# Sharing the scaled residual add of a sandwich block between ScalarE and VectorE

## The chip, the cores and the metric

One core of one Trainium2 chip runs the kernel. The metric is the device time of one execution in microseconds (us). Engines are called as in the profile: PE is TensorE, DVE is VectorE, ACT is ScalarE, POOL is GpSimd, SP is SyncE.

## The reference, cut to what matters

```python
x = L0_attn_x                                     # (4, 1024, 512) f32
x = x + _layernorm(attention(_layernorm(x)))      # windowed attention on tokens of 16 channels
x = x + _layernorm(ffn(_layernorm(x)))            # ffn: silu(x@w_gate*s_gate) * (x@w_up*s_up) @ w_down*s_down
```

The change concerns the end of the second line. The attention's rows of 512 values are normalised (mean and variance of each row) and added to x. The layernorm of that sum is what the feed-forward part reads.

## The kernel before

The 4096 rows are worked on in 8 tiles of 512 rows; in the feed-forward layout a tile is 128 partitions by 4 blocks (`q`, `NQ` = 4) of 512 values. The attention of a tile works in another layout (windows on partitions), so its result goes through device memory: `att_store` (SP) writes it to `scratch` and loads it back into `o1`, in the row layout. The order of 16-element pieces in a row of `o1` is not that of `xr` (the block of x itself): `norm1_add` reads `o1` as `(ae h w)` and adds to `xr` as `(h ae w)`, with w = 16, h = 4, ae = 8.

The steps of a tile t that matter here, by name, engine and line:

- `ffn_norm1`: DVE takes statistics of the four blocks of `o1` (L1158) and forms mean and variance (L976 to L984). POOL turns them into the inverse deviation `frs[:, 0, 0]` and the shift `frs[:, 0, 1]` with three small instructions (L826, L828, L830); the last one raises `f_rs`.
- `norm1_add`: DVE waits for `f_rs` and for `xr`, and adds `o1 * frs` to `xr` with 16 SCALAR_TENSOR_TENSOR instructions of 128 elements, four for each block (L1173).
- `ffn_norm2`: DVE takes statistics of `xr` (L1149), again DVE then POOL.
- `norm2_apply`: ACT writes the normalised rows over `o1` (L736); `fx_transpose`: PE transposes them (L593), ACT and DVE split them into two f16 parts `xhi` and `xlo` (L741, L1183).
- `keep_x1`: ACT adds the shift `frs[:, 0, 1]` to `xr` later (L792).
- The feed-forward part of the tile before runs meanwhile in 16 steps m: `gate` and `up` on PE (L599), silu on ACT (L766), `fuse` on DVE (L1190), `fuse_hi` on ACT (L772), `fuse_lo` on POOL (L926), `down` on PE (L622), three steps later. `ps_gate` and `ps_up` have one bank each, so PE's next `gate` waits for the silu and its next `up` for the `fuse`.

One list of steps gives every engine its order (`body_steps`, `attention_steps`, `walk`); each engine runs its own part of it strictly in that order. In the steady tiles `ffn_norm1` has slot 40, `norm1_add` slot 41, `token_bias` (POOL, L843) and `ffn_norm2` slot 42, `norm2_apply` slot 44. Three slots are one step m. So ACT's order about the change is: copy of the last `qkv` (L713), [slot 41], silu of step 14, `fuse_hi` of step 13, and so on. The first tile runs `norm1_add` ahead of any feed-forward step (`BEFORE`), behind ACT's eight `qkv` copies; the last one has it at slot 43 (`LAST2`). `norm1_add` of tile 1 is in `FIRST`, those of tiles 2 to 5 in the hardware loop over `MIDDLE`, that of tile 6 in the copy of `MIDDLE` behind the loop.

Of the kernel before, what the change touches and what calls it, by code (L numbers as in the profile page):

```python
# [10 lines left out]
WIN = 8  # L11
# [10 lines left out]
NQ = ROWS // P  # L22
# [10 lines left out]
ALU = mybir.AluOpType  # L33
ACT = mybir.ActivationFunctionType
# [12 lines left out]
def sandwich_kernel(nc, x, qkv_w, conv_w0, conv_b0, conv_w1, conv_b1, proj_w, proj_b, ln_w, ln_b,  # L47
                    w_gate, w_up, w_down, s_gate, s_up, s_down, scratch, out):
    with ExitStack() as ctx:
        def sb(name, shape, dt=F32):  # L50
            return ctx.enter_context(nc.sbuf_tensor(name, shape, dt))
# [4 lines left out]
        def sem(name):  # L56
            return ctx.enter_context(nc.semaphore(name))
# [60 lines left out]
        o1 = sb("o1", [P, NQ, W])  # L118
# [4 lines left out]
        frs = sb("frs", [P, 3, 2, NQ])  # L123
# [69 lines left out]
        f_stats = sem("f_stats")  # L193
        f_pool = sem("f_pool")
        f_rs = sem("f_rs")
        xr_sum = sem("xr_sum")
        fx_done = sem("fx_done")
        fx_tr = sem("fx_tr")
# [153 lines left out]
        p, a, b, c = (0, 0), (0, 1), (1, 0), (1, 1)  # L352
# [94 lines left out]
        def _(sp):  # L447
            def load_xb(t, *_):

                need(sp, xt_tr, 4 * t)
                need(sp, xl_done, 4 * t)
                for h in range(WIN):
                    src = x_att[t, h] if isinstance(t, int) else x_att[bass.ds(t, 1), h].rearrange("o k p w -> (o k) p w")
                    sp.dma_start(xb[:, h, :], src).then_inc(s_xb, 16)

            def load_xr(t, *_):

                need(sp, x1_done, t)
                if isinstance(t, int) and t == 0:  # L460
                    sp.wait_ge(w_cast, 2 * KB)
                for hi in range(2):
                    if isinstance(t, int):
                        src = x_ffn[t // 2, t % 2, hi]
                    else:
                        src = x_ffn[bass.ds(t // 2, 1), bass.ds(t % 2, 1), hi].rearrange("b s lo k n -> (b s lo) k n")
                    dst = xr[:, 2 * hi:2 * hi + 2, :].rearrange("p q n -> p (q n)")
                    sp.dma_start(dst, src).then_inc(s_xr, 16)

            def att_store(t, *_):  # L470

                if isinstance(t, int) and t == 0:
                    sp.wait_ge(w_cast, CASTS)

                need(sp, s_out, 32 * (t - 1))
                dst = r_store[t] if isinstance(t, int) else r_store[bass.ds(t, 1)].rearrange("o p c n -> (o p) c n")
                src = ratt[:].rearrange("p c h w -> p c (h w)")
                for hi in range(2):

                    sp.wait_ge(ratt_done, 4 * t + 3 + hi)  # L480
                    part = slice(hi * HB, hi * HB + HB)
                    sp.dma_start(dst[:, part], src[:, part]).then_inc(s_ratt[hi], 16)
                if isinstance(t, int) and t == 1:

                    sp.wait_ge(fx_tr, KB)
                for hi in range(2):

                    sp.wait_ge(s_ratt[hi], 16 * t + 16)
                    for g in range(2):
                        rows = r_load[t, hi, g] if isinstance(t, int) \  # L490
                            else r_load[bass.ds(t, 1), hi, g].rearrange("o r ae n -> (o r) ae n")
                        sp.dma_start(o1[:, 2 * hi + g, :].rearrange("p (ae n) -> p ae n", ae=2 * NQ),
                                     rows).then_inc(s_o1[hi], 16)
# [196 lines left out]
        def _(act):  # L690
# [35 lines left out]
            def square(at, u, ut, uq):  # L726
# [3 lines left out]
                nc.scalar.activation(csq[:, part].rearrange("p h t c -> p (h t c)"),  # L730
                                     cent[:, part].rearrange("p h t c -> p (h t c)"), ACT.Square).then_inc(sq_done, 1)

            def norm2_apply(t, ut, uq):
                act.wait_ge(f_rs, 2 * t + 2)
                for q in range(NQ):
                    nc.scalar.activation(o1[:, q, :], xr[:, q, :], ACT.Identity, bias=frs[:, 1, 1, q:q + 1],  # L736
                                         scale=frs[:, 1, 0, q:q + 1]).then_inc(fx_done, 1)
# [71 lines left out]
            for dst, src in ((sgate, s_gate), (sup, s_up)):  # L809
                act.dma_start(dst[:], src.rearrange("(m p) -> p m", p=P),  # L810
                              allow_slow_non_contiguous=True).then_inc(s_const2, 16)
            walk(act, {"ln1_apply": ln1_apply, "xt_transpose": xt_transpose, "qkv": qkv, "exp": exp,
                       "cat_transpose": cat_transpose, "square": square, "cent_std": cent_std,
                       "norm2_apply": norm2_apply, "fx_transpose": fx_transpose,
                       "gate": gate, "fuse_hi": fuse_hi, "finish_apply": finish_apply,
                       "finish_apply_last": finish_apply_last, "keep_x1": keep_x1,
                       "cast": cast})
# [153 lines left out]
        def _(dve):  # L971
# [190 lines left out]
            def norm1_add(t, ut, uq):  # L1162

                dve.wait_ge(f_rs, 2 * t + 1)
                dve.wait_ge(s_xr, 32 * t + 32)
                for q in range(NQ):

                    sums = xr[:, q, :].rearrange("p (h ae w) -> p h ae w", h=WIN // 2, w=C)  # L1170
                    rows = o1[:, q, :].rearrange("p (ae h w) -> p h ae w", h=WIN // 2, w=C)
                    for h in range(WIN // 2):
                        a = nc.vector.scalar_tensor_tensor(sums[:, h], rows[:, h], frs[:, 0, 0, q:q + 1], sums[:, h],  # L1173
                                                           ALU.mult, ALU.add)
                    a.then_inc(xr_sum, 1)

            def ffn_norm2(t, ut, uq):
                dve.wait_ge(xr_sum, NQ * t + NQ)
# [117 lines left out]
            def scales(t, ut, uq):  # L1296
# [11 lines left out]
                       "softmax": softmax, "pv": pv, "pv_norm": pv_norm,  # L1308
                       "attn_out": attn_out, "proj": proj, "cent_var": cent_var, "cent_out": cent_out,
                       "ffn_norm1": ffn_norm1, "norm1_add": norm1_add, "ffn_norm2": ffn_norm2,  # L1310
                       "fx_transpose": fx_transpose, "fuse": fuse_step, "pv_sum": pv_sum,
                       "finish": finish, "blocks": blocks, "scale_sums": scale_sums, "scale_pow2": scale_pow2,
# [29 lines left out]
```

## Time and profile before

| | us |
|---|---|
| median of 3 runs (lowest, highest) | 1413.1 (1411.92, 1414.27) |
| span of the profiled execution | 1412.0 |
| DVE busy | 1243.1 (88%) |
| PE busy | 1044.9 (74%) |
| POOL busy | 765.3 (54%) |
| ACT busy | 523.5 (37%) |

Busy time counts an instruction from its start to its end, and that includes any time it is held back inside by another engine. The timeline view gives start, duration, engine, line, operation and shapes, and in square brackets the idle time of the engine before it and who ended that.

### The profile page before, as it was taken

Reading aid. Unit: us, or ns where it says so; the run is one execution under the profiler, and the core shown is the slowest. Engines: PE = TensorE matmul, PEld = TensorE weight load, DVE = VectorE, ACT = ScalarE, POOL = GpSimd, SP = SyncE. Lnnn points to the kernel's source line nnn. Section 1 sums busy time; section 2 is a strip of 40 time slices with the busy share of each in tenths; the row PEclk is TensorE's granted clock in tenths of the full one; section 3 lists DMA queues with packets and bytes.
Section 4 is the critical chain, followed back from the end, with each engine's and each line's share of the span. In section 5 each row is a group of like instructions: output and inputs, shape, how many; then the busy total and the mean of one; then the engine's idle time right before and its main releaser. Section 6 shows DMA issues by size and latency. Waiting matters only on the chain. (4 is left out here: it accounts for less than half of the span.)

```text
span 1412.0 us, 14344 instructions
## 1 busy us (share of the span) xinstructions
PE 1044.9 (74%) x4483; PEld 531.0 (38%) x4483; DVE 1243.1 (88%) x1716; ACT 523.5 (37%) x790; POOL 765.3 (54%) x492
## 2 busy tenths in 40 slices
PE   5524368777887688868787778876887688678896
PEld 3312244343443343434343334433444244233442
DVE  4999999999899999999899998999899999975313
ACT  2235335332452434414253324524344143523332
POOL 2555336565576555765456644765557664754322
PEclk9756669889898899979898899988899799889998
DMA  4100200103001210102101030012101020012000
GB/s 128 30 0 13 77 6 24 30 1 89 1 16 45 60 31 1 38 21 59 30 3 57 0 89 1 15 45 59 30 1 46 15 60 1 7 53 60 7 24 30
DMA packets 70266, 46.07 MB, mean 33 GB/s; under 512 B 39616, under 2 KB 64192, under 8 KB 70208
## 3 DMA queue, kind: packets, MB, share of 16 engines
q1 hardware_dynamic: 65344, 45.10, 11.5%
q10 hardware_dynamic: 4864, 0.32, 0.2%
q8 instruction: 22, 0.36, 0.1%
q14 instruction: 36, 0.29, 0.1%
HBM read 28.63 MB, written 16.78 MB: 32 GB/s over the span
## 5 line engine op out<-in xcount | busy, mean ns | idle before, releaser
L599 PE MATMUL ps_up<-xhi,wu 128*128 128x512 f16 x512 | 218.8, 427 | 145.1 <-DVE fuse L1190 144.9
L864 POOL TENSOR_TENSOR sum<-prod 128x1024 f32<-128x1024 f32 x64 | 154.4, 2412 | 171.1 <-DVE prod L1031 171.1
L873 POOL TENSOR_TENSOR sum<-prod 128x1024 f32<-128x1024 f32 x64 | 158.6, 2478 | 156.4 <-DVE prod L1031 156.4
L1031 DVE TENSOR_TENSOR prod<-probs,qkvl 128x512 f32<-128x512 f32 x256 | 240.0, 1000 | 0.0
L1031 DVE TENSOR_TENSOR prod<-qkvl 128x512 f32<-128x512 f32 x256 | 222.2, 927 | 6.3 <-ACT qkvl L713 6.3
L599 PE MATMUL ps_up<-xlo,wu 128*128 128x512 f16 x512 | 218.2, 426 | 0.0
L599 PE MATMUL ps_gate<-xhi,wg 128*128 128x512 f16 x512 | 207.5, 405 | 3.6 <-DVE xlo L1183 3.2
L599 PE MATMUL ps_gate<-xlo,wg 128*128 128x512 f16 x512 | 205.5, 401 | 0.0
L926 POOL TENSOR_TENSOR flo<-fuse,fhi 128x512 f16<-128x512 f32 x128 | 172.8, 1351 | 59.2 <-ACT fhi L772 59.2
L766 ACT ACTIVATE gact<-ps_gate,sgate 128x512 f32<-128x512 f32 x128 | 87.7, 685 | 231.4 <-PE ps_gate L599 231.2
L1190 DVE SCALAR_TENSOR_TENSOR fuse<-ps_up,sup,gact 128x512 f32<-128x512 f32 x128 | 95.3, 744 | 77.0 <-PE ps_up L599 70.4
L1046 DVE TENSOR_TENSOR sum<-sum 128x512 f32<-128x512 f32 x128 | 161.7, 1263 | 0.2 <-POOL sum L873 0.2
L599 PEld LDWEIGHTS ps_up<-xhi,wu 128*128 128x128 f16 x512 | 55.6, 109 | 230.2 <-DVE fuse L1190 167.2
L622 PE MATMUL ps_acc<-wd,fhi 128*128 128x512 f16 x500 | 135.4, 395 | 0.6 <-POOL flo L926 0.6
L622 PE MATMUL ps_acc<-wd,flo 128*128 128x512 f16 x500 | 130.1, 383 | 0.0
L556 PE MATMUL ps_q<-wqkvl,xt 128*128 128x512 f32 x128 | 81.8, 726 | 51.3 <-ACT qkvl L713 48.7
L772 ACT ACTIVATE fhi<-fuse 128x512 f16<-128x512 f32 x128 | 79.7, 623 | 59.9 <-DVE fuse L1190 59.6
L1048 DVE TENSOR_TENSOR probs<-sum 128x256 f32<-128x256 f32 x64 | 87.0, 1359 | 2.2
L556 PE MATMUL ps_t<-wqkvl,xt 128*128 128x512 f32 x128 | 83.2, 737 | 6.1 <-ACT qkvl L713 6.1
L599 PEld LDWEIGHTS ps_gate<-xhi,wg 128*128 128x128 f16 x512 | 54.8, 107 | 66.6 <-issue 16.3
L599 PEld LDWEIGHTS ps_up<-xlo,wu 128*128 128x128 f16 x512 | 54.6, 107 | 62.7 <-issue 21.0
L599 PEld LDWEIGHTS ps_gate<-xlo,wg 128*128 128x128 f16 x512 | 53.0, 104 | 60.4 <-issue 11.6
(169 smaller groups left out, 1719.2 us busy)
## 6 DMA issues: line engine op xcount, KB each, us to landing
xb<-in_L_attn_x SPq DMA_DIRECT2D x64, 128.0 KB, 2.6
xr<-in_L_attn_x SPq DMA_DIRECT2D x16, 512.0 KB
attn_rows<-ratt SPq DMA_DIRECT2D x16, 512.0 KB, 2.9
o<-attn_rows SPq DMA_DIRECT2D x32, 256.0 KB, 3.8
out_x<-o SPq DMA_DIRECT2D x14, 512.0 KB
x<-in_L_ffn_w_gate SPq DMA_DIRECT2D x1, 1024.0 KB, 5.4
xr<-in_L_ffn_w_up SPq DMA_DIRECT2D x1, 1024.0 KB, 7.6
out_x<-o SPq DMA_DIRECT2D x4, 256.0 KB
```

Source lines behind the costliest of these rows:

```text
L556: mm = nc.tensor.matmul(bank(h)[:], xt[:, h, :], wqkvl[:].rearrange("p g t c -> p (g t c)"), start=True, stop=False, skip_group_check=True)
L599: mm = nc.tensor.matmul(ps[:], w[:, k, :], xs[:, k, :], start=(k == 0 and part == 0), stop=(k == KB - 1 and part == 1))
L622: mm = nc.tensor.matmul(ps_acc[q][:], f[:, m % SPLITS, P * q:P * q + P], wd[:, m, :], start=(m == 0 and part == 0), stop=(m == MB - 1 and ...
L766: nc.scalar.activation(gact[:, m % 2, :], ps_gate[:], ACT.Silu, scale=sgate[:, m:m + 1]).then_inc(silu_done, 1)
L772: nc.scalar.activation(fhi[:, m % SPLITS, :], fuse[:, m % 2, :], ACT.Copy).then_inc(fhi_done, 1)
L864: nc.gpsimd.tensor_tensor(dst.rearrange("p (s c) -> p s c", c=4), s[:, :, 0:4], s[:, :, 4:8], ALU.add).then_inc(half_done, 1)
L873: nc.gpsimd.tensor_tensor(dst.rearrange("p (w jc) -> p w jc", jc=4 * HB), s[:, :, 0:4 * HB], s[:, :, 4 * HB:], ALU.add).then_inc(half_done, 1)
L926: nc.gpsimd.tensor_tensor(flo[:, m % SPLITS, :], fuse[:, m % 2, :], fhi[:, m % SPLITS, :], ALU.subtract).then_inc(flo_done, 1)
L1031: a = nc.vector.tensor_tensor(dst, left(g, br, w), right(g, br, w), ALU.mult)
L1046: nc.vector.tensor_tensor(lo, lo, hi, ALU.add).then_inc(att_chain, 1)
L1048: nc.vector.tensor_tensor(dst, one, two, ALU.add).then_inc(att_chain, 1)
L1190: nc.vector.scalar_tensor_tensor(fuse[:, m % 2, :], ps_up[:], sup[:, m:m + 1], gact[:, m % 2, :], ALU.mult, ALU.mult).then_inc(fuse_done, 1)
```

## The change

ACT gets a step `norm1_add` at the same place of the common order: it waits for `f_rs` and multiplies each block of `o1` in place by `frs[:, 0, 0, q]`. It raises a new semaphore `o1_scaled` for each block. DVE no longer waits for `f_rs`; it waits for `o1_scaled` block by block and adds the block to `xr` with one TENSOR_TENSOR over all four `h` pieces at once.

```diff
+            def norm1_add(t, ut, uq):
+                act.wait_ge(f_rs, 2 * t + 1)
+                for q in range(NQ):
+                    nc.scalar.activation(o1[:, q, :], o1[:, q, :], ACT.Copy,
+                                         scale=frs[:, 0, 0, q:q + 1]).then_inc(o1_scaled, 1)
...
             def norm1_add(t, ut, uq):
-                dve.wait_ge(f_rs, 2 * t + 1)
                 dve.wait_ge(s_xr, 32 * t + 32)
                 for q in range(NQ):
+                    dve.wait_ge(o1_scaled, NQ * t + q + 1)
                     sums = xr[:, q, :].rearrange("p (h ae w) -> p h ae w", h=WIN // 2, w=C)
                     rows = o1[:, q, :].rearrange("p (ae h w) -> p h ae w", h=WIN // 2, w=C)
-                    for h in range(WIN // 2):
-                        a = nc.vector.scalar_tensor_tensor(sums[:, h], rows[:, h], frs[:, 0, 0, q:q + 1], sums[:, h],
-                                                           ALU.mult, ALU.add)
-                    a.then_inc(xr_sum, 1)
+                    nc.vector.tensor_tensor(sums, rows, sums, ALU.add).then_inc(xr_sum, 1)
```

## Rows read from the trace of the kernel before

**Rows 1.** The page's first part: busy time, share and instructions of each engine.
```profile
PE 1044.9 (74%) x4483; PEld 531.0 (38%) x4483; DVE 1243.1 (88%) x1716; ACT 523.5 (37%) x790; POOL 765.3 (54%) x492
```
**Rows 2.** Groups by line and shape, DVE: L1173, with mean ns of one.
```profile
L1173 DVE SCALAR_TENSOR_TENSOR xr<-o,frs,xr 128x128 f32<-128x128 f32 x128 | 55.6, 508 | 7.1 <-POOL frs L830 7.0
```
**Rows 3.** Timeline of tile 2's norm1_add, DVE: start us, duration us, instruction.
```profile
506.21 7.15 DVE L1173 SCALAR_TENSOR_TENSOR xr<-o,frs,xr 128x128 f32<-128x128 f32 x16 [1.01 <-POOL frs L830]
```
**Rows 4.** The same 16 instructions in narrow windows: the first, the second, four later ones.
```profile
506.21 1.11 DVE L1173 SCALAR_TENSOR_TENSOR xr<-o,frs,xr 128x128 f32<-128x128 f32 x1 [1.01 <-POOL frs L830]
...
507.25 2.44 DVE L1173 SCALAR_TENSOR_TENSOR xr<-o,frs,xr 128x128 f32<-128x128 f32 x1
...
509.87 1.13 DVE L1173 SCALAR_TENSOR_TENSOR xr<-o,frs,xr 128x128 f32<-128x128 f32 x4
```
**Rows 5.** Timeline of the same stretch, POOL.
```profile
505.87 0.20 POOL L830 TENSOR_TENSOR frs<-fmv,frs 128x4 f32<-128x4 f32 x1
506.02 1.15 POOL L926 TENSOR_TENSOR flo<-fuse,fhi 128x512 f16<-128x512 f32 x1
507.13 2.40 POOL L843 TENSOR_TENSOR xl<-xb,lnb 128x1024 f32<-128x1024 f32 x1
516.77 0.60 POOL L826 TENSOR_TENSOR frs<-fmv,epsx 128x4 f32<-128x4 f32 x1 [7.24 <-DVE fmv L984]
```
**Rows 6.** Timeline of the same stretch, ACT.
```profile
508.13 0.69 ACT L766 ACTIVATE gact<-ps_gate,sgate 128x512 f32<-128x512 f32 x1 [2.86 <-PE ps_gate L599]
...
519.13 2.93 ACT L736 ACTIVATE o<-xr,frs 128x512 f32<-128x512 f32 x4 [9.79 <-POOL frs L830]
```
**Rows 7.** Timeline of the same stretch, PE.
```profile
511.38 0.38 PE L599 MATMUL ps_gate<-xhi,wg 128*128 128x512 f16 x1
...
518.49 0.61 PE L599 MATMUL ps_up<-xhi,wu 128*128 128x512 f16 x1 [5.22 <-DVE fuse L1190]
```
**Rows 8.** Views of single lines: duration ns as min/median/max, starts, shape.
```profile
L1208 DVE TENSOR_TENSOR o<-o,x x4: 684/693/694, 1402.4 to 1406.1; 128x512 f32<-128x512 f32 x4
...
L792 ACT ACTIVATE x<-xr,frs x32: 707/710/722, 267.2 to 1350.9; 128x512 f32<-128x512 f32 x32
```
**Rows 9.** Timeline, DVE: four products back to back, and one add with strided reads.
```profile
182.74 2.50 DVE L1031 TENSOR_TENSOR prod<-probs,qkvl 128x512 f32<-128x512 f32 x4
...
177.56 0.61 DVE L1048 TENSOR_TENSOR probs<-sum 128x256 f32<-128x256 f32 x1
```
**Rows 10.** Timeline of tile 0's norm1_add: DVE, POOL, and ACT's last qkv copy.
```profile
185.33 6.42 DVE L1173 SCALAR_TENSOR_TENSOR xr<-o,frs,xr 128x128 f32<-128x128 f32 x16
...
185.31 2.35 POOL L873 TENSOR_TENSOR sum<-prod 128x1024 f32<-128x1024 f32 x1
...
187.87 0.60 ACT L713 ACTIVATE qkvl<-ps_t 128x512 f32<-128x512 f32 x1 [0.48 <-PE ps_t L561]
```
**Rows 11.** Timeline of tile 7's norm1_add: DVE and POOL.
```profile
1293.36 6.06 DVE L1173 SCALAR_TENSOR_TENSOR xr<-o,frs,xr 128x128 f32<-128x128 f32 x16 [0.98 <-POOL frs L830]
...
1293.28 2.32 POOL L926 TENSOR_TENSOR flo<-fuse,fhi 128x512 f16<-128x512 f32 x2
```
**Rows 12.** Timeline, PE: up of step 15 behind norm1_add, tiles 1 and 5.
```profile
354.96 0.61 PE L599 MATMUL ps_up<-xhi,wu 128*128 128x512 f16 x1 [5.62 <-DVE fuse L1190]
...
1013.65 0.61 PE L599 MATMUL ps_up<-xhi,wu 128*128 128x512 f16 x1 [5.33 <-DVE fuse L1190]
```
**Rows 13.** Busy time by stretch; the third number from the end is the granted clock.
```profile
353.00:361.00 8.00, 6.04 (x15) 2.19 (x16) 5.96 (x9) 4.02 (x6) 6.35 (x6) 0.57 0.01 2
...
516.00:524.00 8.00, 5.51 (x23) 2.66 (x24) 6.45 (x14) 4.09 (x7) 5.76 (x5) 0.79 0.08 24
```
**Rows 14.** Timeline, DVE: first L1183 behind norm1_add, tiles 1, 2, 5 and 6.
```profile
362.56 0.69 DVE L1183 TENSOR_TENSOR xlo<-ps_q,xhi 128x512 f16<-128x512 f32 x1 [2.61 <-ACT xhi L741]
...
524.56 0.69 DVE L1183 TENSOR_TENSOR xlo<-ps_q,xhi 128x512 f16<-128x512 f32 x1 [1.08 <-ACT xhi L741]
...
1021.29 0.69 DVE L1183 TENSOR_TENSOR xlo<-ps_q,xhi 128x512 f16<-128x512 f32 x1 [2.66 <-ACT xhi L741]
...
1182.67 0.69 DVE L1183 TENSOR_TENSOR xlo<-ps_q,xhi 128x512 f16<-128x512 f32 x1 [1.42 <-ACT xhi L741]
```

More of the change, by code:

```diff
@@ L195, in sandwich_kernel @@
         f_rs = sem("f_rs")
+        o1_scaled = sem("o1_scaled")
         xr_sum = sem("xr_sum")
@@ L813, in _ @@
                        "cat_transpose": cat_transpose, "square": square, "cent_std": cent_std,
-                       "norm2_apply": norm2_apply, "fx_transpose": fx_transpose,
+                       "norm1_add": norm1_add, "norm2_apply": norm2_apply, "fx_transpose": fx_transpose,
                        "gate": gate, "fuse_hi": fuse_hi, "finish_apply": finish_apply,
```

## The prediction, made before the changed kernel was run

> **What bounds the kernel now.** I read the page's first part for the loads, then the group of the changed line, then the timeline about one steady `norm1_add`, engine by engine. DVE is busy 88% of the span, ACT 37% [rows 1], so work moved from DVE to ACT goes from the fuller to the emptier engine. A share is no proof; the place is.
>
> The 128 instructions of L1173 cost 55.6 us, 508 ns in the mean [rows 2]. In a steady tile they take 7.15 us [rows 3]. They are not alike: the first takes 1.11 us, the second 2.44, and four later ones 1.13 together, so (1.13 - 0.34) / 3 = 0.26 from start to start if one alone takes 0.34 [rows 4]. The two long ones lie where POOL runs `flo` (506.02 to 507.17) and `token_bias` (507.13 to 509.53) [rows 5]: DVE's instruction with two SBUF inputs gets in at the end of the first, the next is held back until the second is over. DVE finishes at 506.21 + 7.15 = 513.36.
>
> Who waits for it? PE's `up` of step 15 has been idle for 5.22 us and is released by the `fuse` behind this add [rows 7]. POOL idles 7.24 us until the statistics of the sum are there [rows 5]. ACT idles 9.79 us until POOL's answer [rows 6]. So at this spot all three others stand still behind DVE's chain add, statistics, `fuse`, and a microsecond saved or lost in the add moves the whole program by one, unless it meets another limit later. All eight tiles have this form except tile 0, where no feed-forward step runs yet.
>
> **The change, part by part.**
>
> *ACT, added.* Four Copy instructions of 128x512 with one per-partition scale. The nearest row is L792, same shape with one per-partition operand: 0.710 us [rows 8]. Four L736 with two such operands take 2.93 us [rows 6]; that one alone takes about 0.80, so (2.93 - 0.80) / 3 = 0.71 from start to start and 0.09 of overlap, which gives 0.62 for mine. `f_rs` comes at 506.07 (L830, 505.87 + 0.20). ACT is idle from 505.27 to 508.13 [rows 6], so it starts at about 506.1: blocks ready at 506.85, 507.5, 508.1, 508.7. Behind it in ACT's queue stand the silu of step 14, now at 508.6 rather than 508.13, and `fuse_hi` 13. PE wants that silu for the `gate` of step 15 at 511.38 [rows 7], and POOL wants `fuse_hi` only behind `ffn_norm2`. So the ACT work costs nothing here: 2 us of slack hide 0.5. Without that cover it would cost 0.5 us per tile. Copy follows silu elsewhere on ACT without a table load, so none is added.
>
> *DVE, removed and added.* Out go 16 instructions at 0.26 = 4.2 us from start to start. In come 4 TENSOR_TENSOR of 512 elements. L1208, the same operation on contiguous blocks, takes 0.69 alone [rows 8]; four L1031, whose inputs are many-dimensional, with runs of 8 elements, take 2.50 [rows 9], so (2.50 - 0.69) / 3 = 0.60 from start to start. My reads are in runs of 16; I take 0.60, four rows 2.5 us with the last one's end. A bound from above is the add L1048, which reads single elements with gaps: 0.61 for 256 [rows 9], or 1.2 us for 512.
>
> *The rule against the row.* The Trainium skill (Vector Engine (DVE) Microarchitecture Reference, "Measured stream behaviour on trn2") gives 1.04 ns a column plus about 75 ns an instruction. By that 16 small ones would cost 16 x 0.208 = 3.3 us, four large 2.4, and the change would save 0.9 us a tile and not 1.7; seven tiles would give about 1407, an estimate from that page. The row is 0.26 us for 128 columns, and it decides; the same page ("Points that are easy to get wrong") says that SCALAR_TENSOR_TENSOR with two f32 SBUF sources runs at half the rate, which fits the row.
>
> *The new wait, against POOL.* DVE's first block is ready at 506.9, not 506.1, while `flo` runs to 507.17. As the first small one does now, it gets in between `flo` and `token_bias`. POOL is then held for the rest of that one instruction (as its L826 of 4 elements takes 0.60 beside a DVE add [rows 5] and 0.20 alone), about 0.4 us more, so `token_bias` ends near 509.9. Blocks 2 to 4 follow: end near 509.9 + 0.69 + 2 x 0.60 - 0.2 = 511.6. If the first block misses the gap, all four start at 509.5 and end at 509.5 + 2.5 = 512.0. Gain 513.36 less that: 1.4 to 1.8, and I take 1.6. What is queued behind the new wait on DVE is `ffn_norm2` and `pv_sum`, which waited for the add anyway.
>
> *Tile 7.* Two `flo` fill POOL from 1293.28 to 1295.60, DVE ends at 1299.42 [rows 11]. Four blocks behind the second: 1295.6 + 2.5 = 1298.1, or 1297.7 if one slips in: gain 1.3 to 1.7.
>
> *Tile 0.* DVE now runs 185.33 to 191.75, ACT's last `qkv` copy ends at 188.47 [rows 10], and the new step stands behind it. Blocks are ready from 189.1 in steps of 0.62, the last at 190.95, and DVE ends at 191.65. Gain 0; here ACT takes the place of POOL as what holds DVE.
>
> *PE's clock behind the add.* With the idle of 5.62 and 5.33 us in tiles 1 and 5 [rows 12] (tile 3 is the same), the granted clock over eight microseconds is 0.57, in tile 2 after 5.22 us it is 0.79 [rows 13]. PE's matmuls take 0.61 at the level of 1.2 GHz. DVE then waits 2.61 and 2.66 us for the first L1183, against 1.08 and 1.42 in tiles 2 and 6 [rows 14]. After the change PE idles about 1.6 us less, less than in any tile of now. So the three long slow stretches may become short: 3 x 1.3 = 3.9 us at most; clock stretches may also move and do harm elsewhere. I take 2.1, with 0 and 4 as ends.
>
> *Sum.* Tiles 1 to 7: 7 x 1.6 = 11.2 (9.6 to 12.4). Tile 0: 0. Clock: 2.1 (-1 to 4). Together 13.3. Against the profiled execution's own span 1412.0 that is 1398.7; it lies 1.1 below the median of the runs, so for the median 1413.1 - 13.3 = 1399.8.
>
> **Rivals.**
>
> *Swallowed later (about 1411 to 1413).* A later limit gives the gain back: the loads of `o1`, the clock, the loop. For: in tile 7 alone DVE waits for the load of `o1`. Against: those loads start from the chain that moves too, and PE, POOL and ACT all wait at the add itself.
>
> *DVE gets ahead of `token_bias` with all four blocks (about 1386).* If POOL can't get in between them, DVE ends when ACT does: 508.7 + 0.7 = 509.4, a gain of 4.0 in tiles 1 to 6 and about 1.6 in tile 7, 25.6 with nothing for the clock. Against: now POOL gets in behind the first small instruction though the next is ready [rows 4].
>
> *Slower: the three-dimensional add runs at the strided rate (about 1423).* At L1048's 0.61 for 256 elements a block costs 1.2 and four 4.9: end 509.5 + 4.9 = 514.4, a loss of 1.1 in seven tiles and 2 in tile 0 (189.1 + 4.9 = 194.0 against 191.75), 10 in all, and 1423 with the clock no better. It decides above (513.36 - 509.53) / 4 = 0.96 us a block. Against: L1031 with runs of 8 is at 0.60.
>
> *The change does nothing for DVE since waiting, not work, fills the 7.15.* 3.1 of the 7.15 us are POOL's and remain. That is in the sum already; it would be the whole truth only if ACT delivered the blocks slower than 0.96 us each. L792 says 0.71.
>
> **Chances.** Forecast 0.80; swallowed or partly so, within 0.2% 0.07 and with a small gain 0.05; ahead of POOL 0.04; slower 0.04. A difference of 0.2% (2.8 us) is about what a measurement of this kernel can tell from none. So faster 0.89, same 0.07, slower 0.04. The forecast's own range is 1396 to 1404; with the partly swallowed gain and the clock's other turns I give 1393 to 1406.
>
> **What would show it.** Right: L1173's 16 instructions become four with 0.69 us for an undisturbed one, the last ending 5.4 to 5.9 us after `f_rs` in tiles 1 to 6 (now 7.3); POOL's `token_bias` longer by 0.4; silu 14 later by 0.5 and PE's `gate` 15 not; PE's idle ahead of `up` 15 near 3.6 us; in tile 0 DVE idle for ACT and the same end; a tile shorter by about 2 us from one `norm1_add` to the next. Wrong: blocks over 0.96 us, ACT instructions over 0.9 us or a table load beside them, POOL held for several blocks, or PE waiting for the silu of step 14.

## The result, and the profile after

| | before | after |
|---|---|---|
| median of the runs, us | 1412.95 (4 runs, 1411.92 to 1414.27) | 1394.17 (4 runs, 1389.33 to 1396.03) |
| span of the profiled execution, us | 1412.0 | 1394.0 |
| ratio to before, 95% interval | | 0.9858, 0.9838 to 0.9878 |

The same kernel, run later beside others, gave 0.983 (0.9809 to 0.9852). By the medians the change saves 18.8 and 24.7 us, where 13.3 were forecast. The first result lies at the lower edge of the range 1393 to 1406 (0.9858 of 1413.1 is 1393.0), and the second lies below it (0.983 of 1413.1 is 1389.1). The direction was right; a part of the gain was missing from the sum.

The page's first part, to be held against [rows 1], and the groups of the two changed lines, against [rows 2]:

```profile
PE 1034.4 (74%) x4483; PEld 530.1 (38%) x4483; DVE 1221.9 (88%) x1620; ACT 543.7 (39%) x822; POOL 767.4 (55%) x492
...
L1179 DVE TENSOR_TENSOR xr<-o,xr 128x512 f32<-128x512 f32 x32 | 34.9, 1150 | 16.0 <-ACT o L737 16.0
...
L737 ACT ACTIVATE o<-o,frs 128x512 f32<-128x512 f32 x32 | 20.5, 710 | 8.0 <-POOL frs L837 8.0
```

DVE is 21 us less busy and ACT 20 us more. DVE's 55.6 us of L1173 became 34.9 us of L1179, with 16.0 us of idle time ahead of them.

The timeline of tile 2's `norm1_add` after the change, DVE, POOL, ACT and PE in turn, to be read beside [rows 3 to 7] (start, duration, instruction, idle before it; the second line is the first add alone):

```profile
506.58 4.83 DVE L1179 TENSOR_TENSOR xr<-o,xr 128x512 f32<-128x512 f32 x4 [1.66 <-ACT o L737]
...
506.58 0.87 DVE L1179 TENSOR_TENSOR xr<-o,xr 128x512 f32<-128x512 f32 x1 [1.66 <-ACT o L737]
...
505.58 0.20 POOL L837 TENSOR_TENSOR frs<-fmv,frs 128x4 f32<-128x4 f32 x1
505.74 1.16 POOL L933 TENSOR_TENSOR flo<-fuse,fhi 128x512 f16<-128x512 f32 x1
506.85 2.80 POOL L850 TENSOR_TENSOR xl<-xb,lnb 128x1024 f32<-128x1024 f32 x1
...
505.82 2.56 ACT L737 ACTIVATE o<-o,frs 128x512 f32<-128x512 f32 x4 [1.07 <-POOL frs L837]
508.29 0.67 ACT L773 ACTIVATE gact<-ps_gate,sgate 128x512 f32<-128x512 f32 x1
...
516.54 0.39 PE L600 MATMUL ps_up<-xhi,wu 128*128 128x512 f16 x1 [3.79 <-DVE fuse L1194]
```

`f_rs` comes at 505.78 and the adds end at 511.41: 5.6 us behind it, where it was 7.3. The same difference, 1.67 us, is found in tiles 1 to 7. That is the part that was forecast. It makes 11.7 us of the 18.0 between the two spans. The next fence has what was not forecast: the end of the loop's first round on DVE, before and then after.

```profile
529.35 0.68 DVE L1183 TENSOR_TENSOR xlo<-ps_t,xhi 128x512 f16<-128x512 f32 x1
532.37 1.23 DVE L1111 TENSOR_TENSOR attn<-attn,ssum 128x1024 f32<-128x1024 f32 x1 [2.33 <-issue]
```
```profile
527.75 0.68 DVE L1187 TENSOR_TENSOR xlo<-ps_t,xhi 128x512 f16<-128x512 f32 x1
528.35 1.22 DVE L1118 TENSOR_TENSOR attn<-attn,ssum 128x1024 f32<-128x1024 f32 x1
```

L1183 is DVE's last instruction ahead of the branch back and L1111 its first behind it. Before, DVE stood still for 2.33 us between them, released by nothing that the profile shows ("issue"). The view of waits of before has it three times, once for each branch taken (the group's us in total, times, longest us):

```profile
DVE attn L1111 <- issue: 7.1, 3, 2.5
```

After the change that group is gone from the view. The page's third part shows what went with it, the queue that loads instructions (packets, MB), before and after:

```profile
q14 instruction: 36, 0.29, 0.1%
```
```profile
q14 instruction: 21, 0.17, 0.0%
```

There are 15 packets fewer, of 0.29 MB / 36 = 8 KB each. The trace also has the start of every packet. Before, one starts in each of the three idle stretches, about 0.4 us into it (530.43, 696.26, 861.15), and five come in each later round of the loop, which makes the 15. After the change none starts between 525.97 and 1010.90. The change had not touched the head of the loop or its branch; it had made DVE's program shorter, by 12 instructions for each `norm1_add`.

### The profile page after: what moved, and what is told of

The parts are those of the page before. It is cut to its first block and busy times, and to the rows that moved or that the text cites. A ratio compares the mean times of both kernels' runs of the same rounds, so it can differ in the third digit from the quotient of the medians.

```text
span 1394.0 us, 14280 instructions
## 1 busy us (share of the span) xinstructions
PE 1034.4 (74%) x4483; PEld 530.1 (38%) x4483; DVE 1221.9 (88%) x1620; ACT 543.7 (39%) x822; POOL 767.4 (55%) x492
## 5 line engine op out<-in xcount | busy, mean ns | idle before, releaser
L600 PE MATMUL ps_up<-xhi,wu 128*128 128x512 f16 x512 | 214.2, 418 | 134.4 <-DVE fuse L1194 134.2
L600 PE MATMUL ps_up<-xlo,wu 128*128 128x512 f16 x512 | 214.3, 419 | 0.0
L1053 DVE TENSOR_TENSOR sum<-sum 128x512 f32<-128x512 f32 x128 | 158.7, 1240 | 0.0
```

The source lines that it names most:

```text
L600: mm = nc.tensor.matmul(ps[:], w[:, k, :], xs[:, k, :], start=(k == 0 and part == 0), stop=(k == KB - 1 and part == 1))
L1053: nc.vector.tensor_tensor(lo, lo, hi, ALU.add).then_inc(att_chain, 1)
```

## The experiments

**Move the old loop, change nothing else.**

```diff
             nc.vector.memset(ones[:], 1.0).then_inc(wvt_done, 1)
+            for _ in range(128):
+                dve.wait_ge(wvt_done, 1)
```

> The kernel before, with 128 satisfied waits (64 instructions) at the very start of VectorE's program; its arithmetic and its loop body (332 VectorE instructions) are unchanged, only their place in the program moves. Theory 1 (place): VectorE's code is fetched in 8 KB pieces of 128 instructions, and in the kernel before the loop touches a fourth piece at its end, so the first has to be fetched again behind the branch back: 2.3 to 2.5 us of idle time with no releaser, three times. 64 instructions later the loop lies in three pieces: that idle time falls below 0.5 us each, the fetches within the loop vanish, and the program gains about 7 us, ratio near 0.995. Theory 2 (length of the body): nothing changes, ratio 1.000. Theory 3 (the 20 us come from the add and PE's clock alone): nothing changes either.

Measured: ratio 0.9955 (0.9934 to 0.9976). The same place in its timeline, and its instruction queue:

```profile
533.42 0.68 DVE L1183 TENSOR_TENSOR xlo<-ps_t,xhi 128x512 f16<-128x512 f32 x1
534.02 1.22 DVE L1111 TENSOR_TENSOR attn<-attn,ssum 128x1024 f32<-128x1024 f32 x1
```
```profile
q14 instruction: 23, 0.18, 0.0%
```

The idle time is gone though not one instruction of the loop differs; 64 instructions that do nothing make the kernel 6.5 us faster (1407.2 against 1413.7). No packet starts between 509.56 and 1032.25. Theories 2 and 3 fall.

**The changed kernel at the old place, and 12 instructions further on.** The first puts place and length back, the second only the place.

```diff
                     nc.vector.tensor_tensor(sums, rows, sums, ALU.add).then_inc(xr_sum, 1)
+                for _ in range(24):
+                    dve.wait_ge(wvt_done, 3)
```

> The changed kernel with 24 satisfied waits (12 instructions) behind each norm1_add of VectorE, so that both the loop's place and its length on VectorE (332) are those of the kernel before. Theories 1 and 2: the 2.3 to 2.5 us of idle time behind the branch return three times, and the time is about 7 us more than the changed kernel's, ratio to before near 0.991. Theory 3: only the 12 waits' own time, under 0.6 us a tile, ratio near 0.987.

Measured: 0.9906 (0.9878 to 0.9933). The second:

```diff
             nc.vector.memset(ones[:], 1.0).then_inc(wvt_done, 1)
+            for _ in range(24):
+                dve.wait_ge(wvt_done, 1)
```

> The changed kernel with 24 satisfied waits (12 instructions) at the very start of VectorE's program, its loop body of 320 instructions unchanged. The changed kernel's loop ends within a few instructions of a piece's boundary; 12 later it crosses it. Theory 1 (place): the idle time of 2.3 to 2.5 us behind the branch returns three times, ratio to before near 0.991. Theory 2 (length): the body is still 320, no idle time, ratio near 0.986.

Measured: 0.9882 (0.9858 to 0.9906). Its first branch back on DVE, and its view of waits:

```profile
528.50 1.22 DVE L1118 TENSOR_TENSOR attn<-attn,ssum 128x1024 f32<-128x1024 f32 x1 [2.65 <-issue]
```
```profile
DVE attn L1118 <- issue: 7.5, 3, 2.7
```

The spans of the two are 1399.1 and 1398.3, against 1394.0 and 1391.5 for two profiles of the changed kernel. The times alone would leave both unclear, as their intervals touch or overlap that of the changed kernel (0.9838 to 0.9878); the idle time decides, and it is back in both, with the body of 320 too. Counted in DVE's program, the loop stands behind 533 instructions and ends with the 865th before (idle), behind 597 and with the 929th (none), behind 509 and with the 829th after (none), behind 521 and with the 841st (idle). The changed kernel's freedom from this wait is thus luck of a few instructions.

**A prefetch hint in the old kernel's loop.**

```diff
-            with eng.Fori(1, TILES - 3) as t:
+            with nc.Fori(1, TILES - 3, engines=[eng.engine],
+                         hint_back_edge=eng.engine == mybir.EngineType.DVE) as t:
```

Measured: 0.9969 (0.9952 to 0.9986), and the idle time is gone:

```profile
529.02 0.68 DVE L1184 TENSOR_TENSOR xlo<-ps_t,xhi 128x512 f16<-128x512 f32 x1
529.62 1.22 DVE L1112 TENSOR_TENSOR attn<-attn,ssum 128x1024 f32<-128x1024 f32 x1
```

Place and length are those of before but for the hint itself. Together with the packets in the idle stretches this shows that the wait was for the loop's own code. One detail was expected otherwise: the packets of the instruction queue fell from 36 to 22, with none between 505.42 and 1027.97, so the hint does not only make the fetch earlier, it saves nearly all fetches within the loop. Why is open.

**What the add itself gained from.** The prediction left two readings of L1173's 0.26 us: half the rate, or a higher fixed cost. First ScalarE scales as in the change, but DVE's adds are small again:

```diff
-                    nc.vector.tensor_tensor(sums, rows, sums, ALU.add).then_inc(xr_sum, 1)
+                    for h in range(WIN // 2):
+                        a = nc.vector.tensor_tensor(sums[:, h], rows[:, h], sums[:, h], ALU.add)
+                    a.then_inc(xr_sum, 1)
```

> The changed kernel with VectorE's four adds of 512 elements cut back into 16 of 128; ScalarE scales as in the change, the loop's place and length are those of the kernel before. If SCALAR_TENSOR_TENSOR with two f32 inputs from SBUF runs at half the rate, a plain add of 128 takes about 0.21 us from start to start (0.26 before) and norm1_add ends about 6.5 us behind f_rs (7.3 before, 5.6 after): 0.7 us gained a tile, 5 in all, with the loop's idle time kept: ratio near 0.996. If the fixed cost of an instruction is what counts, an add takes 0.26 too and the ratio is 0.999 to 1.001.

Measured: 0.9959 (0.9945 to 0.9973), the adds ending 6.45 us behind `f_rs`. Then the fused instruction is kept, but made large, without ScalarE. This kernel leaves out the reordering of the pieces, so it serves for times alone:

```diff
-                    for h in range(WIN // 2):
-                        a = nc.vector.scalar_tensor_tensor(sums[:, h], rows[:, h], frs[:, 0, 0, q:q + 1], sums[:, h],
-                                                           ALU.mult, ALU.add)
-                    a.then_inc(xr_sum, 1)
+                    nc.vector.scalar_tensor_tensor(xr[:, q, :], o1[:, q, :], frs[:, 0, 0, q:q + 1], xr[:, q, :],
+                                                   ALU.mult, ALU.add).then_inc(xr_sum, 1)
```

> The kernel before, with VectorE's 16 fused instructions of 128 elements made into 4 fused ones of 512 over contiguous rows; this leaves out the reordering of the 16-element pieces. ScalarE does nothing more. VectorE's program is as long as in the change, so the idle time behind the loop's branch goes in any case (7 us). Theory half rate (two f32 inputs from SBUF cost a fused instruction two cycles an element): a block takes about 1.14 us from start to start, norm1_add ends 7.3 to 8 us behind f_rs, ratio 0.994 to 0.998. Rival, the fixed cost of 16 instructions is what the change saved: a block takes 0.6 us, norm1_add ends near 5.4, ratio 0.986, without any work of ScalarE.

Measured: 0.9843 (0.9811 to 0.9876). The timelines, small plain adds first (the last 14 of tile 2), then large fused ones (the last three of tile 0):

```profile
506.92 2.90 DVE L1180 TENSOR_TENSOR xr<-o,xr 128x128 f32<-128x128 f32 x14
```
```profile
188.75 2.06 DVE L1170 SCALAR_TENSOR_TENSOR xr<-o,frs,xr 128x512 f32<-128x512 f32 x3
```

With single durations of 0.277 and 0.742 us these give (2.90 - 0.28) / 13 = 0.202 and (2.06 - 0.74) / 2 = 0.66 from start to start. So:

| from start to start, us | 128 columns | 512 columns | per column, ns | fixed |
|---|---|---|---|---|
| TENSOR_TENSOR | 0.202 | 0.602 | 1.04 | 0.07 |
| SCALAR_TENSOR_TENSOR, scalar from a tile | 0.263 | 0.662 | 1.04 | 0.13 |

Both run at one column in 1.04 ns. The first run had agreed with the half rate to the digit and did not tell it from a fixed cost; the second does, and the half rate falls. The fused instruction costs 0.06 us more each, at either length. On this way the 1.67 us a tile are 0.84 for plain adds in place of fused ones (7.29 - 6.45, measured) and 0.83 for 12 fixed costs of 0.07 fewer. On the other way, the large fused ones end 5.73 us behind `f_rs` and the change's adds 5.62: merging 16 fused instructions into 4 gives 1.56 of the 1.67 alone. ScalarE's scaling is not what the gain rests on.

**ScalarE's part alone.** DVE as before; ScalarE scales into a tile that nobody reads.

```diff
+            def norm1_add(t, ut, uq):
+                act.wait_ge(f_rs, 2 * t + 1)
+                for q in range(NQ):
+                    need(act, o1_scaled, NQ * t + q)
+                    nc.scalar.activation(spare[:], o1[:, q, :], ACT.Copy,
+                                         scale=frs[:, 0, 0, q:q + 1]).then_inc(o1_scaled, 1)
```

> The kernel before, with ScalarE's four Copy instructions of the change added at the same place of its order, behind the same wait for f_rs, but writing to a spare tile that nobody reads; VectorE keeps its 16 instructions and its own wait. If ScalarE's part is free, as the prediction said (it fills 2.5 of the 2.9 us for which ScalarE idles there, and TensorE has 2 us to spare before it wants the silu of step 14), the ratio is 0.999 to 1.001 and norm1_add still ends 7.3 us behind f_rs. Rival: the wait at the head of ScalarE's queue delays the silu and with it TensorE: 0.5 us or more a tile, ratio 1.003 or above.

Measured: 0.9995 (0.9981 to 1.0009). Each Copy here also waits for the one before it, so the four take 2.98 us and not 2.56. The silu of step 14 starts at 509.22, 3.0 us behind `f_rs` where it was 2.1, and the time does not change:

```profile
506.33 2.98 ACT L739 ACTIVATE spare<-o,frs 128x512 f32<-128x512 f32 x4 [0.92 <-POOL frs L840]
509.22 0.67 ACT L776 ACTIVATE gact<-ps_gate,sgate 128x512 f32<-128x512 f32 x1
```

**The scaling back on DVE, complete.** The large fused instruction was used above over contiguous rows. For a complete kernel of that kind the loads put the pieces into the right order already, in runs of 64 bytes where they were 256:

```diff
-                        sp.dma_start(o1[:, 2 * hi + g, :].rearrange("p (ae n) -> p ae n", ae=2 * NQ),
-                                     rows).then_inc(s_o1[hi], 16)
+                        dst = o1[:, 2 * hi + g, :].rearrange("p (h ae w) -> p h ae w", h=WIN // 2, w=C)
+                        for h in range(WIN // 2):
+                            sp.dma_start(dst[:, h], rows[:, :, C * h:C * h + C]).then_inc(s_o1[hi], 16)
```

> The kernel before, complete, without ScalarE's part: the loads into o1 are cut in four by h and put the 16-element pieces into the order of xr (64-byte pieces where they were 256), so that VectorE can use the 4 fused instructions of 512 of the run before. If ScalarE's scaling is not what the gain rests on, norm1_add ends 5.7 us behind f_rs in tiles 1 to 6, the idle time behind the loop's branch is gone and the ratio is 0.984 to 0.987. Rival: the loads in small pieces come late (tile 7 already waits 3.7 us for one), VectorE waits for them in every tile, and the ratio is above 0.990.

Measured: 0.9902 (0.9871 to 0.9932), neither of the two. Tiles 1 to 6 behave as forecast (5.74 us behind `f_rs`). The loss is in tile 7, where DVE waits for the loads. The waits of DVE for these loads, before and in this run:

```profile
DVE fst L1158 <- DMA o<-attn_rows: 4.5, 2, 3.7
```
```profile
DVE fst L1159 <- DMA o<-attn_rows: 12.7, 2, 8.2
```

That is 8.2 us more, at once on the path. Here ScalarE's scaling earns its place: not as the cheaper multiplication, but as what goes with a plain add that reads the pieces in their old order at full speed (0.60 us a block) and leaves the loads as they were. No run has a large fused instruction with the reordered read, so that rival is open.

**GpSimd out of the way.** Of the 4.83 us of the adds, some 2.2 are POOL's `token_bias` between the first and the third: the second add takes 2.84 us, where an undisturbed one takes 0.68.

```diff
                 t, g = at
+                if g == 1 and not on_vector(at):
+                    pool.wait_ge(xr_sum, NQ * t)
                 pool.wait_ge(xn_done, 2 * t + 2)
```

> The changed kernel, with GpSimd's token_bias of slot 42 made to wait until norm1_add is done (xr_sum), so that its 2.4 us run beside VectorE's statistics, which read one input, and not between VectorE's adds. Theory: GpSimd holds VectorE's two-input instructions back, 2.3 us of the 4.8 us of norm1_add in tiles 1 to 6. Then the add ends about 3.5 us behind f_rs instead of 5.6, token_bias takes 2.4 us again, and 6 x 2.1 = 12 us are gained: ratio near 0.978. Rival: the collision only moves, to the small statistics instructions or to the products behind them, and the ratio stays at 0.985 to 0.987.

Measured: 0.9723 (0.9695 to 0.9752), 39 us less than before, and 1376.4 against 1391.4 us for the changed kernel beside it. Run again beside the two orders of the load:

> The changed kernel with token_bias behind the add, once more beside the two others: ratio 0.972, and VectorE's wait for the first xlo 0.2 us in most tiles, since TensorE idles too short ahead of the up of step 15 for its clock to fall.

Measured: 0.9715 (0.9661 to 0.977). DVE, POOL and PE in its profile:

```profile
498.60 2.95 DVE L1181 TENSOR_TENSOR xr<-o,xr 128x512 f32<-128x512 f32 x4 [1.66 <-ACT o L737]
501.58 2.47 DVE L1158 BATCH_NORM_STATS2 fst<-xr 128x6 f32<-128x512 f32 x4
...
501.68 2.35 POOL L852 TENSOR_TENSOR xl<-xb,lnb 128x1024 f32<-128x1024 f32 x1 [2.48 <-DVE xr L1181]
...
506.68 0.39 PE L600 MATMUL ps_up<-xhi,wu 128*128 128x512 f16 x1 [2.34 <-DVE fuse L1196]
...
511.86 0.69 DVE L1189 TENSOR_TENSOR xlo<-ps_q,xhi 128x512 f16<-128x512 f32 x1 [0.18 <-ACT xhi L748]
```

`token_bias` now runs beside DVE's statistics. Those read one tensor and take 2.47 us as ever, and `token_bias` takes 2.35 and not 2.80. The adds end 3.5 to 3.7 us behind `f_rs`. The collision did not move, it went; this is the fastest kernel of the study. It gained more than the forecast 0.978, because DVE's wait for the first `xlo` also fell, from 1.4 to 0.2 us in five of the six tiles (more on this below).

With the loads in order as well:

> That kernel with GpSimd's token_bias behind norm1_add as well. If both hold, norm1_add ends about 3.2 us behind f_rs (four blocks at 0.66 and the rest of one flo), and the ratio is near that of the changed kernel with token_bias behind (0.972). Rival: the loads are late, ratio 0.978 or more.

Measured: 0.9785 (0.9754 to 0.9816): the forecast's rival, with the adds at 3.7 us behind `f_rs` and again the late loads of tile 7.

**The changed kernel once more.**

> The changed kernel once more, beside the others on the same chip: ratio 0.986. What the clock does in its profile tells how much of the difference between the two profiles is chance: the waits behind the add should again be the short ones (1.4 us) in tiles 1 to 6, while the start (tile 0's f_rs at 185 or 188 us) and the tail (112.6 or 114.5 us behind the last add) may fall either way.

Measured: 0.983 (0.9809 to 0.9852). In its profile tile 0's `f_rs` comes at 185.5, in the first one of the changed kernel at 188.0 and before at 185.3; the short waits for `xlo` are there again (1.2 to 1.4 us).

## Why the prediction was right and wrong

The step that failed is the sum. It added the adds, tile 0 and PE's clock, and put what happens at the loop's branch at nothing, without a reason. The runs showed 7.1 us there, DVE's three waits for its own code. The term of the adds was right; the clock's term was right in kind only.

*The add: right, in its parts.* Forecast were 0.62 us a block on ScalarE, the first block let in ahead of `token_bias`, POOL held 0.4 us longer for that one, an end 5.4 to 5.9 us behind `f_rs`. The rows show (2.56 - 0.71) / 3 = 0.62, the first add of 0.87 us, `token_bias` at 2.80 for 2.40, and 5.6. In tiles 1 to 7 that is 7 x 1.67 = 11.7 us for a forecast of 11.2. Silu 14 starts 2.5 us behind `f_rs` for 2.1 before: the forecast half microsecond, and hidden; ScalarE's part alone measured as nothing (0.9995, 0.9981 to 1.0009). Tile 0 gained 0.1 us for a forecast of 0, as DVE waits there for ScalarE, which is behind its `qkv` copies.

*The loop: missing.* The sum had no term for the program's own place and length. DVE's program has 24 instructions fewer ahead of the loop and 12 fewer in it, and 7.1 us of "issue" went. The group of waits stood in the view of before; I read it nowhere, as no step of the change touched L1111. The prediction named the loop only among the things that might swallow the gain. With this term the forecast would have been 1392.7. One of its own signs tells of the gap: a tile was to be shorter by about 2 us from one `norm1_add` to the next, and it was shorter by 2.9 to 5.3, with the branch back in the three of 3.8, 5.3 and 4.1.

The Trainium skill has the rule (Runtime: NRT & Kernel Launch, "Instruction fetch mechanics"): an engine holds two blocks of its code, prefetch is sequential, and a taken branch to a target outside them stalls for a fetch. The traces agree with the stall, at 2.3 to 2.7 us a branch. They differ in the size of a block for these engines: that section says 16 KB, while this queue fetches 8 KB at a time. And a whole loop of 320 DVE instructions stays without a fetch from 525.97 to 1010.90.

*PE's clock: right in kind, and partly chance.* The forecast took 2.1 us, with the long slow stretches of tiles 1, 3 and 5 becoming short. Tile 2 after the change: the busy time of a stretch that starts 2 us ahead of `up` 15 (third number from the end: granted clock), and the first `xlo`. Then tiles 2 and 3 of the kernel with `token_bias` behind the add, second profile:

```profile
514.54:522.54 8.00, 6.00 (x24) 2.90 (x25) 5.99 (x9) 4.23 (x7) 6.26 (x6) 0.79 0.18 59
...
522.96 0.69 DVE L1187 TENSOR_TENSOR xlo<-ps_q,xhi 128x512 f16<-128x512 f32 x1 [1.43 <-ACT xhi L748]
```
```profile
504.68:512.68 8.00, 5.93 (x31) 3.07 (x32) 6.82 (x11) 5.37 (x9) 6.26 (x6) 1.00 0.44 131
...
662.44:670.44 8.00, 6.00 (x24) 2.90 (x25) 5.99 (x10) 4.23 (x7) 6.26 (x6) 0.79 0.45 131
```

DVE's waits for the first `xlo` sum to 11.7 us in tiles 1 to 6 before and 8.4 after: 3.2 us gained. PE's idle time ahead of this `up` is 4.6 to 5.6 us before, 3.5 to 4.2 after (forecast: near 3.6), and 1.5 to 2.3 with `token_bias` moved. The clock of such a stretch is 0.57 in tiles 1, 3 and 5 and 0.79 in the others before; 0.79 in all six after; and 1.00 in five of them with `token_bias` moved. The order fits a clock that falls more with a longer idle time, but idle time alone does not decide. The two tiles shown have 2.34 and 2.32 us of it, at 1.00 and 0.79, and tiles 2, 3 and 4 with the large fused instructions have 4.48, 4.47 and 4.49 us, at 0.79, 0.79 and 0.58. What else decides was not varied, so the cause of this term stays open, and that the long stretches of before became short is in part luck. Two stretches went the other way in the profile after. Tile 0's `f_rs` came 2.7 us later, at a PE clock of 0.59 from 150 to 190 us where it was 0.70 before, though the change has no work ahead of it. And in the last feed-forward part PE fell to 1.2 GHz (0.63 us a matmul and not 0.38) for a moment where it had not before:

```profile
1306.30 0.63 PE L600 MATMUL ps_gate<-xhi,wg 128*128 128x512 f16 x1
```

The time from the last add to the end was 1.8 us longer (114.5 for 112.6). The first did not come again in the second profile of the changed kernel (185.5); the second did (114.4), and in the other kernels with its plain add as well (114.3 to 114.6).

*The balance.* 11.7 (add) + 7.1 (loop) + 3.2 (clock behind the add) - 2.6 (start) - 1.8 (tail) = 17.6 of the 18.0 us between the spans. The forecast had 11.2 + 2.1. So the clock in all gave -1.2 us in this profile (3.2 - 2.6 - 1.8) for 2.1: that term was missed too, and only the loop's 7.1 carried the result beyond the forecast. That the first result touches the range's lower edge confirms nothing about the loop.

*The page's rule on the fixed cost.* The prediction held 75 ns an instruction against the row's 0.26 us, and took the half rate of another section as an explanation. The row rightly decided the sum. The explanation was wrong: a plain add costs 0.07 us fixed, as "Measured stream behaviour on trn2" of the Trainium skill's Vector Engine (DVE) Microarchitecture Reference says, the fused one with its scalar from a tile 0.13, and neither runs at half the rate here.

*The rivals.* "Swallowed later" happened nowhere but in the tail. DVE did not get ahead of `token_bias`; the three-dimensional read costs nothing (0.60 us a block, as the contiguous one). Two figures of the rivals were off by their own rows, with no effect on the sum: a gain of 25.6 gives 1387.5 for the median and not 1386, and POOL's share of the 7.15 us is 2.9 and not 3.1 (the first two instructions take 3.40 to the start of the third, less 2 x 0.26).

## What to carry to other kernels

An edit that shortens or lengthens an engine's program ahead of a hardware loop, or in it, can change whether the loop's code is fetched again in each round. Look for "issue" behind the branch and count the packets of the instruction queue before comparing two kernels, and try a prefetch hint on the branch. Where DVE and POOL both work with two SBUF inputs, ask whether a long DVE duration is POOL's. Moving the POOL work beside a DVE instruction with one input gained more here (15 us, 1.1% beyond the change) than making the DVE work cheaper (11.7 us). Merge small instructions before moving their work to another engine: 16 into 4 alone was 1.56 of the 1.67 us a tile.

## What the runs showed of the hardware

- A taken branch back on DVE cost 2.3 to 2.7 us when the loop's head was fetched again (before, and four more profiles), and otherwise nothing: the next instruction starts with no gap (after, and eight more). Twelve instructions that do nothing, far from the loop, switched it on in the changed kernel; 64 switched it off in the old one.
- SCALAR_TENSOR_TENSOR with a scalar from a tile costs 0.06 us more than TENSOR_TENSOR, at 128 columns (0.263 and 0.202 us from start to start) and at 512 (0.662 and 0.602).
- Where POOL and DVE both had two-input work queued about `norm1_add`, one DVE instruction got in between two of POOL's, be it 128 or 512 columns long, and POOL's was longer by about what it waited: 2.40 us behind a small one, 2.80 behind a large one, 2.35 beside DVE's statistics.
